# Row scores of attention on four 32-row tiles of the matrix engine, and the first reciprocals in SBUF

## The reference, cut to what matters

```python
x = x + _L0_xattn_ref(_layernorm(x), ctx, ctx, position_ids, Wq, Wk, Wv, Wo)
x = x + _L0_ffn_ref(_layernorm(x), A_w, B_w, Wq_w, keys)
...
scores = jnp.einsum('bhqd,bhkd->bhqk', q, k) * scale
probs = jax.nn.softmax(scores, axis=-1)
ctx = jnp.einsum('bhqk,bhkd->bhqd', probs, v)
```

## Time and profile before

| | |
|---|---|
| time, median of 3 runs | 170.12 us (169.83 to 170.38) |
| span of the profiled execution (first to last instruction) | 168.1 us |
| median less span | 2.0 us |
| TensorE matmuls busy | 162.7 us (97%) |
| TensorE weight loads busy | 129.9 us (77%) |
| VectorE busy | 134.9 us (80%) |
| ScalarE / GpSimd busy | 89.8 / 91.1 us |
| row scores, L1320 | 192 matmuls |
| maxima, L921 | 32 reductions, 689 ns each |

### The profile page before, as it was taken

How to read it: one execution, slowest core, us unless ns; L and a number is a source line. 1 busy time by engine, 2 the same in 40 slices (tenths; PEclk the granted TensorE clock), 3 DMA queues, 4 the chain that set the end, 5 groups by cost and what they waited for, 6 DMA issues and landing times.

```text
span 168.1 us, 4082 instructions
## 1 busy us (share of the span) xinstructions
PE 162.7 (97%) x1437; PEld 129.9 (77%) x1437; DVE 134.9 (80%) x394; ACT 89.8 (53%) x212; POOL 91.1 (54%) x113
## 2 busy tenths in 40 slices
PE   7999999899999999999999999999999999999993
PEld 2657786678878787879887987879888866889883
DVE  1969886986998899799887998699884988767752
ACT  3588989899656362723538234732349154333210
POOL 5479999899799654805952099206440303512100
DMA  5999952313203010210212000100010001000013
GB/s 173 361 415 388 408 161 62 129 21 105 66 7 118 4 62 0 78 52 0 64 59 69 4 0 0 64 4 0 0 66 0 0 4 62 4 0 4 0 62 125
DMA packets 6739, 13.46 MB, mean 80 GB/s; under 512 B 832, under 2 KB 1216, under 8 KB 6464
## 3 DMA queue, kind: packets, MB, share of 16 engines
q1 hardware_dynamic: 6432, 12.95, 22.7%
q10 hardware_dynamic: 288, 0.27, 0.5%
HBM read 11.11 MB, written 2.10 MB: 79 GB/s over the span
## 4 chain that ended last, share of the span: by engine, by line
PE 52%; POOL 26%; issue 11%; DVE 5%; ACT 2%; DMA 2%; POOLq 0%; ACTq 0%; DVEq 0%
PE ps_w L1234 8%; PE ps_w L1235 7%; PE ps_w L1239 7%; PE ps_t L1247 4%; POOL am_lo L330 3%; POOL k_bd_hi L374 3%; POOL wo_lo L330 3%; PE ps_s L1320 3%; PE ps_s L1339 3%; POOL wq_lo L330 3%; POOL b_lo L330 2%; PE ps_t L1234 2%; PE ps_t L1239 2%; PE ps_t L1235 2%; POOL k_bd_lo L374 2%
## 5 line engine op out<-in xcount | busy, mean ns | idle before, releaser
L921 DVE TENSOR_REDUCE ps_s<-ps_s 128x8 f32<-128x512 f32 x32 | 21.0, 689 | 0.6 <-PE ps_s L1320 0.3
L398 POOL TENSOR_TENSOR late<-late,gate 128x512 f32<-128x512 f32 x7 | 7.6, 1084 | 24.2 <-issue 17.3
L383 POOL TENSOR_TENSOR oT_lo<-o_n,oT_hi 128x512 fp32r<-128x512 f32 x8 | 10.4, 1296 | 15.7 <-ACT oT_hi L611 15.7
L603 ACT ACTIVATE eT<-ps_s 128x512 f32<-128x512 f32 x32 | 17.0, 600 | 3.4 <-PE ps_s L1345 3.4
L1234 PE MATMUL ps_w<-am_hi,x2T_hi 128*128 128x288 f32 x48 | 14.3, 320 | 0.0
L1235 PE MATMUL ps_w<-am_lo,x2T_hi 128*128 128x288 f32 x48 | 13.1, 295 | 0.0
L1234 PE MATMUL ps_w<-b_hi,zT_hi 128*128 128x512 f32 (+1 forms) x28 | 10.7, 389 | 0.0
L1227 PE MATMUL ps_w<-wq_hi,xT_hi 128*128 128x512 f32 x26 | 10.7, 411 | 0.0
L1234 PEld LDWEIGHTS ps_w<-am_hi,x2T_hi 128*128 128x128 f32 x48 | 9.0, 187 | 2.1 <-ACT late L635 0.4
L1235 PE MATMUL ps_w<-b_lo,zT_hi 128*128 128x512 f32 (+1 forms) x28 | 10.4, 376 | 0.0
L653 ACT ACTIVATE zT_hi<-ps_t 128x512 fp32r<-128x512 f32 x7 | 4.2, 598 | 11.4 <-PE ps_t L1247 11.4
(11 more groups left out here) (256 smaller groups left out, 537.2 us busy)
## 6 DMA issues: line engine op xcount, KB each, us to landing
x_sb<-x SPq DMA_DIRECT2D x8, 256.0 KB, 6.7
cT_in<-cT SPq DMA_DIRECT2D x7, 256.0 KB, 2.8
out<-res SPq DMA_DIRECT2D x7, 256.0 KB, 2.0
wq_sb<-wq SPq DMA_DIRECT2D x4, 256.0 KB, 5.4
late<-wo SPq DMA_DIRECT2D x1, 1024.0 KB, 7.7
am_sb<-aT SPq DMA_DIRECT2D x1, 1024.0 KB, 8.8
b_sb<-bT SPq DMA_DIRECT2D x1, 1024.0 KB, 7.2
xT_raw<-xT SPq DMA_DIRECT2D x4, 256.0 KB, 2.9
```

The lines of the kernel that those rows point to most:

```text
L383: pool.tensor_tensor(oT_lo[:], o_n[:].rearrange("p (b r q) -> p r b q", b=2, r=REP), oT_hi[:].bitcast(F32), ALU.subtract).then_inc(oT_lo_o ...
L603: act.activation(eT[:, c].rearrange("p b n -> p (b n)"), ps_s[:, c, :], ACT.Exp)\
L921: dve.tensor_reduce(neg_top[:, b, HALF_H * half:HALF_H * (half + 1), :], ps_s[:, 2 * (1 - b) + half, :].rearrange("p (r h k) -> p h r k", ...
```

## The change

`quad_scores(t)` takes the place of `scores(t, 0)` and `scores(t, 1)` for tiles 0 to 6 (`quad_rows`). It has 48 matmuls on four 32-row tiles, each with 128 moving columns, in 12 groups of four; each group writes all four banks of `ps_s`, and b and `rp` choose the columns. The semaphore `s_ps` rises by 2 at the end, so that `top(t, 0)` waits for all the scores. The reductions are still four of 512 elements; they read a column range of all four banks. `neg_top` for these tiles lies in bank 0, in the order (r, b, h). `scores` remains for tile 7, and `top(7, b)` with it. The reciprocals of tiles 0, 1 and 2 go to `inv_late` in SBUF, as those of tiles 6 and 7 did, and the wait of tiles 1 to 3 on `o_step` is for the transpose only (3 t - 2), at the start of the stage.

```diff
--- before.py
+++ after.py
@@ -143,7 +143,6 @@
 
 
         ps_s = pb("ps_s", [P, 4, D])
-        neg_top = ps_s[:, 2, 0:4 * KVH].rearrange("p (b h r) -> p b h r", b=2, r=2)
         ps_w0, ps_w1 = pb("ps_w0", [P, D]), pb("ps_w1", [P, D])
         ps_t = pb("ps_t", [P, 2, D])
         ps_t0, ps_t1 = ps_t[:, 0, :], ps_t[:, 1, :]
@@ -156,6 +155,14 @@
             return ps_t if late_tile(t) else ps_s[:, 0:2, :]
 
         ROUTE = ps_s[:, :, 0:E]
+
+        def quad_rows(t):
+            return t < T - 1
+
+        def neg_top_of(t):
+            if quad_rows(t):
+                return ps_s[:, 0, 0:4 * KVH].rearrange("p (r b h) -> p b h r", b=2, r=2)
+            return ps_s[:, 2, 0:4 * KVH].rearrange("p (b h r) -> p b h r", b=2, r=2)
 
         def z_bank(t, half):
             if t == T - 1:
@@ -173,9 +180,7 @@
             return (xT_raw[:].rearrange("p k q -> p (k q)"), res[:], z_sb, zg)[k]
 
         def inv_of(t):
-            if t >= T - 2:
-                return inv_late[:]
-            return (ps_t1 if late_tile(t) else ps_s[:, 0, :])[:, 0:2 * HD].rearrange("p (h u) -> p h u", h=2)
+            return ps_t1[:, 0:2 * HD].rearrange("p (h u) -> p h u", h=2) if late_tile(t) else inv_late[:]
 
         def x2T_of(t):
             return (x2T_hi, x2T_lo) if t < T - 1 else (xT_hi, xT_lo)
@@ -912,6 +917,20 @@
                                   ALU.subtract).then_inc(qT_lo_ok, 1)
 
             def top(t, b):
+                neg_top = neg_top_of(t)
+                if quad_rows(t):
+                    if b == 0:
+                        dve.wait_ge(s_ps, 2 * t + 2)
+                        if t >= 1:
+                            dve.wait_ge(m_lo_ok, t)
+                    for rp in range(2):
+                        if b == 0 and rp == 1:
+                            dve.wait_ge(max_ok, 4 * t + 1)
+                        at = 2 * P * b + P * rp
+                        dve.tensor_reduce(neg_top[:, b, :, rp].rearrange("p (c h) -> p c h", h=2),
+                                          ps_s[:, :, at:at + P].rearrange("p c (h k) -> p c h k", h=2),
+                                          AX.X, ALU.max, negate=True).then_inc(max_ok, 1)
+                    return
                 dve.wait_ge(s_ps, 2 * t + b + 1)
                 if t >= 1 and b == 0:
                     dve.wait_ge(m_lo_ok, t)
@@ -923,7 +942,7 @@
                                       AX.X, ALU.max, negate=True).then_inc(max_ok, 1)
 
             def m_parts(t):
-                raw = neg_top.rearrange("p b h r -> p r (b h)").unsqueeze(2)\
+                raw = neg_top_of(t).rearrange("p b h r -> p r (b h)").unsqueeze(2)\
                     .broadcast_to([P, 2, PAIRS, 2 * KVH])
                 dve.wait_ge(max_ok, 4 * t + 4)
                 if t >= 1:
@@ -1304,15 +1323,36 @@
                 pe.wait_ge(kT_lo_ok, t + 1)
                 turn(qT_bank(t), q_r, REP).then_inc(qT_ps, 1)
 
+            def quad_scores(t):
+                pe.wait_ge(qT_hi_ok, t + 1)
+                pe.wait_ge(qT_lo_ok, t + 1)
+                pe.wait_ge(k_bd_ok, 2 * t + 2)
+                if t >= 1:
+                    pe.wait_ge(exp_ok, 4 * t)
+                    if not late_tile(t - 1):
+                        pe.wait_ge(o_step, 3 * t - 2)
+                for b in range(2):
+                    for rp in range(2):
+                        for n, (q, k) in enumerate(((qT_hi, k_bd_hi), (qT_hi, k_bd_lo), (qT_lo, k_bd_hi))):
+                            for c in range(PAIRS):
+                                rows = slice(QUAD * c, QUAD * (c + 1))
+                                at = 2 * P * b + P * rp
+                                mm = pe.matmul(ps_s[:, c, at:at + P],
+                                               q[rows, t % 2, b, 2 * rp:2 * rp + 2, :].rearrange("p r q -> p (r q)"),
+                                               k[rows, t % 2, b, 2 * (c % 2):2 * (c % 2) + 2, :]
+                                               .rearrange("p h k -> p (h k)"),
+                                               start=(n == 0), stop=(n == 2))
+                mm.then_inc(s_ps, 2)
+
             def scores(t, b):
                 pe.wait_ge(qT_hi_ok, t + 1)
                 pe.wait_ge(qT_lo_ok, t + 1)
                 pe.wait_ge(k_bd_ok, 2 * t + 2)
                 if t >= 1:
-                    if b == 0 or late_tile(t - 1):
+                    if b == 0:
                         pe.wait_ge(exp_ok, 4 * t)
                     else:
-                        pe.wait_ge(o_step, 3 * t if t < T - 1 else 3 * t - 2)
+                        pe.wait_ge(o_step, 3 * t - 2)
                 for rp in range(2):
                     for n, (q, k) in enumerate(((qT_hi, k_bd_hi), (qT_hi, k_bd_lo), (qT_lo, k_bd_hi))):
                         for half in range(2):
@@ -1450,8 +1490,7 @@
                 q_high_part(1, [0, 1])
                 q_low_part(1, [0])
                 pe.wait_ge(route_ok, 1)
-                scores(0, 0)
-                scores(0, 1)
+                quad_scores(0)
                 turn_k(1)
                 q_low_part(1, [1])
                 project_q(1, [2, 3]).then_inc(q_ps, 1)
@@ -1473,8 +1512,7 @@
                 project_q(2, [3]).then_inc(q_ps, 1)
                 pe.wait_ge(qT_lo_ok, 2)
                 turn_xh(3)
-                scores(1, 0)
-                scores(1, 1)
+                quad_scores(1)
                 pe.wait_ge(v_st_ok, 3)
                 out_high(0)
                 out_low_part(0, [0, 1])
@@ -1509,8 +1547,7 @@
                 project_kv(p)
                 if f >= 0:
                     project_q(p, [2])
-                scores(n, 0)
-                scores(n, 1)
+                quad_scores(n)
                 if f >= 0:
                     pe.wait_ge(x2T_lo_ok, i)
                     turn_zg(f)
```

## The result

The changed kernel takes **172.99 us**, the median of four runs (172.41 to 173.95); the kernel before, on the same chip beside it, 169.98 (169.71 to 170.38). The ratio is **1.0178, with an interval of 1.0135 to 1.0222**: slower by 3.0 us. The forecast was slower by 0.6, its range ended at 171.6, and 172.99 lies outside it.

The account below looks back on a forecast made before the run. Bound: early, a serial chain through the maxima of tiles 0 and 1; from 67.50 us, TensorE nearly alone. +0.57 + 0.30 - 0.3 = +0.57 us on a 168.1 us span; from the 170.12 median, 170.7 us, range 169.3 to 171.6.

Parts of the forecast that it names:

- Reciprocals in SBUF: VectorE's multiplication by the reciprocals: 417 ns with them in PSUM, 422 in SBUF; six such, 0.03 us, booked as 0.
- theory P: Held in the experiments: with both operands in SBUF, VectorE's multiplication by the reciprocals waits for a GpSimd operation running beside it.
- The 0.10 left for lateness that grows on its way: Chance 0.10 for a slower reduction over four banks or GpSimd pushed past another due time: 171 to 172 us.
- The first wait: VectorE's first maxima wait for all the scores: +0.57 us at tile 0, +0.30 us more at tile 1.
- The step of a group: TensorE's row scores: a group of four follows the last after 0.111 us, against 0.119 for a pair before.
- rival A: Row scores: columns decide, weight loads overlap fully, step 0.06 to 0.065 us; faster, 168.2 us; chance 0.12.
- C: Row scores: narrow fp32r matmuls run at plain float32's pace, 0.216 us per 128 columns; 178.4 us; chance 0.06.
- The late tiles: Tiles 4, 5 and 6, where TensorE is the chain: three times 0.10 us saved, -0.3 us.
- Rival B: Before 67.5 us, GpSimd's weight splits are the bound and absorb 0.87 us of early lateness; 169.8 us; chance 0.22.
- The maxima over four banks: VectorE's maxima, as many reductions over as many elements, read over four banks instead of one: taken as 0 extra.

Follow-up runs that it names:

- the execution of 197.9 us: One execution of the kernel before with only the reciprocals of tiles 0 to 2 moved to SBUF, at a granted clock of 0.76 throughout: 197.9 us, left out of the ratios.
- the warm kernel: The changed kernel with eight matmuls on a constant put in TensorE's idle stretch before tile 0's output projection: 172.52 us, ratio 1.0142.
- the warm kernel with tile 1 free: The warm kernel with GpSimd's split b_lo moved behind the low part of tile 1's output: 171.44 us, ratio 1.0087.

## Why the prediction was wrong

**The step that failed: "Reciprocals in SBUF".** It took 417 ns against 422 and booked 0. The number of `inv_late` came from four instances at 138.5 to 143.0 us, where GpSimd has nothing running beside them, and that had been taken to hold for all. Of the instances that were moved, those at 28.86 and 41.30 us lie where GpSimd runs its splits. With both operands in SBUF one of a tile's two multiplications takes 1.29 to 1.63 us there, and the other 0.41 to 0.66 (in the run with the split moved, 0.62 and 0.41 at tile 0, which had only the end of a split beside it, and 1.29 and 1.50 at tile 1; in the execution of 197.9 us 0.90 and 0.41 at tile 0). With the reciprocals in PSUM each takes 0.42 beside the same splits. Tile 0 alone: +1.4 us. In all profiles together 17 multiplications with both operands in SBUF began while a split was running. They took 0.54 to 1.63 us, and every one of them ended 0.28 us after the split (0.278 to 0.285): the split's end sets theirs. In the kernel after, VectorE's 1627 ns, begun at 29.53 beside an `am_lo` begun at 29.29, end 0.28 us after it. What it is in the hardware that holds VectorE back no run shows; the "port" and the "lock" of theory P were my guess; the runs show when it happens and what it costs.

**The term that was missing: the clock.** The lateness at tile 0 left TensorE idle for 2.02 us, and the products after it ran at a granted clock of 0.50, 0.42 us from one to the next, where it is 0.23 in the warm kernel at 1.0 (33.82, 34.05). +1.4 us, by the warm kernel against the changed one, and again by the totals of the warm kernel with tile 1 free and the changed one (+1.63 against +3.0). I had costed lateness as lateness and not asked whether an idle stretch that grows costs clock behind it. The 0.10 left for lateness that grows on its way (171 to 172) named GpSimd as one that is late, not as one that blocks VectorE.

**The first wait: right.** +0.57 predicted, 0.60 measured; TensorE's stall at `turn_m(0)` grew from 0.34 to 0.95 us. At tile 1 +0.30 was predicted. The wait alone, in 64-row tiles, shows 0.42 idle there, so it is real; in the changed kernel the scores of tile 1 ended at 30.69 while the blocked multiplication held VectorE to 31.16, and it is hidden.

**The step of a group: right.** 0.112 us on average behind the second group, against the 0.111 taken, and rivals A (0.06) and C (0.216) fall with it. The four weight loads of a group start within 0.01 us of one another, as rival A had it, and the loads of the next group 0.11 us later (29.12, 29.23, 29.34 at tile 1 of the kernel after), never before the matmuls of the group ahead. That the weight load sets the step fits the 0.10 to 0.11 read off; no run varied the load, so it is argued and not shown.

**The late tiles: right in kind.** -0.3 predicted; -0.25 in the profiled span of the changed kernel, and -0.11 to -0.14 per tile between scores. Rival B falls: the wait alone passed through whole.

**The maxima over four banks: right.** 2.63 and 2.60 us for the four, as before. Tiles 2 and 3 cost nothing in the changed kernel.

The sum that holds: 0.6 + 1.4 + 1.4 - 0.3 = 3.1, less 0.46 for the earlier start in the profiled execution, is 2.6 on a span of 168.1, and 170.7 was its span; in medians it is +3.0. The 0.3 us of a wait hidden behind the block would come back without it.

Open: two of the changed kernel's six runs do not fit this sum. That of 173.95 us had a granted clock of 1.0 in its whole span; with the block at tile 1 in place of the clock it should have taken some 172.6, as the warm kernel did (a run of the reciprocals alone, 174.07 at 1.0, is as far off). That of 173.69 had 0.98, about twice the loss of the profiled run's 0.99. No profile of such a run was taken, and a later start of tile 0's row scores, up to 1 us, could be part of it.

## What to carry to other kernels

An operand moved from PSUM to SBUF has to be priced at the places where the operation runs, by what GpSimd does beside it there (0.42 us alone and up to 1.63 beside a split here); the mean or median of undisturbed instances says nothing of it. Look at the longest instance of a group, and at what becomes late and idle behind it: TensorE's idle stretch of 2.02 us cost as much again in clock here (1.4 us, at a granted clock of 0.50 for 3.4 us). Time won at one place brings the next operations forward, possibly into work that they had missed: the runs that cleared tile 0 or kept the clock lost 0.9 to 2.0 us at tile 1. And narrower row tiles paid here only where TensorE is the chain, and little (0.112 us for a step of 0.119); where a consumer starts on the first half of the output, the order that finishes everything last costs more than it saves, so use it on the late tiles alone.

## What was not expected of the hardware

- A VectorE multiplication of 128x256 float32 with both operands in SBUF: 0.42 us alone; begun beside a running split of GpSimd it ended 0.28 us after the split, in 17 of 17 cases, and took up to 1.63. With one operand in PSUM: 0.42 beside the same split. GpSimd's `am_lo` took 1.43 us when it was not contested and 1.59 when VectorE's multiplication ran as it began.
- Clearing tile 0 brought tile 1's multiplications 2.4 us forward, beside two splits that had been there all along, and the two lost 2.0 us.
- TensorE's granted clock fell to half at idle stretches of 2.02 and 1.64 us, 0.3 us before the end of the first and 0.5 us after the end of the second; it held through 1.22 and 0.43 us with matmuls between, and through single ones of up to 1.06 us. One stretch of 3.4 us at the lower level cost 1.4 us.
- A group of four 32-row matmuls with 128 columns steps in 0.112 us, against 0.119 for a pair of 64-row ones with 256: half the columns, 6% less time.
